# A fused four-layer transformer block: two late weights' lower parts on GpSimd, modulation's products later, new orders for the first five turns

## What is computed

```python
# stage A: per-batch adapter, layer norm with a conditioned bias, then the first half of a DiT block
Wd_b = Wd + 0.1 * (cond @ Wdd.T + bdd).reshape(B, 128, 256)      # a weight of its own for each batch
Wu_b = Wu + 0.1 * (cond @ Wdu.T + bdu).reshape(B, 256, 128)
x = x + relu(x @ Wd_b.T + bd) @ Wu_b.T + bu
x = (layernorm(x) * w + b + tanh(cond @ lin_w.T + lin_b)) * w + b
g1, b1, g2, b2, a1, a2 = split(silu(t + side) @ W_c.T + b_c)      # modulation
q, k, v = split((layernorm(x) * g1 + b1) @ W_qkv.T + b_qkv)       # 16 heads of 16
# stage B: attention over 256 positions
o = softmax(q @ k.T / 4) @ v
# stage C
x = x + (o @ W_o.T + b_o) * a1
x = x + (gelu((layernorm(x) * g2 + b2) @ W_f1.T + b_f1) @ W_f2.T + b_f2) * a2
# stage D: RMS norm, gated GELU, rows quantised to 8 bits, ternary weight
u = (x * scale * rsqrt(mean(x*x) + eps)) @ up_w.T
y = quantise(val * gelu(gate)) @ ternary(down_w).T + x
```

## Time and profile before

| | us |
|---|---|
| median of 3 runs | 933.14 (932.55 to 935.09) |
| the profiled execution | 935.74, its span 933.9 |
| PE busy in the span | 843.1 (90%) |
| DVE, ACT, POOL busy | 565.4, 510.9, 231.2 |
| DMA, mean over the span | 127 GB/s; 344 to 366 in the first 70 us |

### The profile page before, as it was taken

How to read it: one execution, slowest core, us unless ns; L and a number is a source line. 1 busy time by engine, 2 the same in 40 slices (tenths; PEclk the granted TensorE clock), 3 DMA queues, 4 the chain that set the end, 5 groups by cost and what they waited for, 6 DMA issues and landing times.

```text
span 933.9 us, 15916 instructions
## 1 busy us (share of the span) xinstructions
PE 843.1 (90%) x5852; PEld 633.5 (68%) x5852; DVE 565.4 (61%) x1063; ACT 510.9 (55%) x796; POOL 231.2 (25%) x333
## 2 busy tenths in 40 slices
...
GB/s 344 365 366 252 248 138 124 148 80 122 62 203 38 135 97 114 120 78 156 47 187 47 188 47 188 46 173 61 154 76 142 65 127 80 104 80 25 24 12 12
DMA packets 58477, 118.48 MB, mean 127 GB/s; under 512 B 6336, under 2 KB 15936, under 8 KB 55696
## 3 DMA queue, kind: packets, MB, share of 16 engines
...
## 4 chain that ended last, share of the span: by engine, by line
PE 74%; issue 9%; DMA 7%; DVE 4%; ACT 2%; SPq 2%; POOL 2%; POOLq 0%; DVEq 0%; ACTq 0%
PE bank L486 30%; PE bank L692 11%; PE pair_s L653 6%; PE pair_s L618 5%; PE pair_t L639 5%; PE pair_t L486 4%; DMA hyp<-in_hyper 3%; PE bank L737 3%; PE bank L664 3%; PE bank L567 2%; PE bank L729 1%; PE bank L561 1%; DVE oq L1145 1%; DMA wc<-in_cols 1%; PE bank L574 1%
## 5 line engine op out<-in xcount | busy, mean ns | idle before, releaser
L851 ACT ACTIVATE Pr<-pair_t 128x1024 f32<-128x1024 f32 x128 | 131.3, 1026 | 125.2 <-PE pair_t L639 121.5
L1121 DVE TENSOR_REDUCE nmax<-pair_s 128x4 f32<-128x1024 f32 x128 | 155.8, 1217 | 34.5 <-PE pair_s L618 33.9
L692 PE MATMUL bank<-wf,G 128*128 128x256 f32 x512 | 123.0, 387 | 0.1
L486 PE MATMUL bank<-wup_hi,hD_hi 128*128 128x512 f32 x256 | 109.4, 427 | 4.8 <-POOL hD_lo L1316 4.1
L1344 POOL TENSOR_TENSOR x<-x,xcr 128x512 f32<-128x512 f32 x16 | 20.5, 1281 | 358.1 <-DVE x L1179 358.1
L692 PEld LDWEIGHTS bank<-wf,G 128*128 128x128 f32 x512 | 93.3, 190 | 15.5 <-issue 0.2
L486 PE MATMUL bank<-wup_lo,hD_hi 128*128 128x512 f32 x256 | 102.0, 398 | 0.0
L486 PE MATMUL bank<-wup_hi,hD_lo 128*128 128x512 f32 x256 | 101.9, 398 | 0.0
L618 PE MATMUL pair_s<-Kp,Qp 64*128 64x256 f32 x512 | 66.1, 337 | 21.7 <-DVE nmax L1121 13.0
L895 ACT ACTIVATE gl<-bank,rsD 128x512 f32<-128x512 f32 x64 | 44.1, 689 | 63.6 <-PE bank L486 63.4
L1189 DVE SCALAR_TENSOR_TENSOR hd<-bank,rsD,gl 128x512 f32<-128x512 f32 x64 | 47.9, 748 | 46.2 <-PE bank L486 34.7
...
## 6 DMA issues: line engine op xcount, KB each, us to landing
hyp<-in_hyper SPq DMA_DIRECT2D x16, 1024.0 KB, 10.2
...
```

The source lines that it names most:

```text
L486: mm = pe.matmul(dst, l, r, start=first and i == 0, stop=last and i == 2)
L692: mm = pe.matmul(bank[5][:, r * D:(r + 1) * D], G[:, k, r * P:(r + 1) * P], wf2[:, k, :], start=k == 0, stop=k == FT - 1)
L851: act.activation(Pr[:, p % 4, :, :].rearrange("p a n -> p (a n)"), pair_t[:, :, :].rearrange("p a n -> p (a n)"), ACT.Exp, scale=DH ** -0. ...
L1121: dve.tensor_reduce(nmax[:, n % 2, :, p % GP, :], pair_s[:, :, :].rearrange("p a (r n) -> p a r n", r=RT), AX.X, ALU.max, negate=True).the ...
```

## The change

Four things change together. W.fa and W.up's lower parts move from DVE to POOL, in 4 and 8 pieces of 128x512 each. Modulation's products move behind the generation's passes 2 and 3 on PE (wo's product too), and DVE copies slot 3 of the first round earlier. All five lists of turns 0 to 4 are new. SP waits, ahead of A.qs and A.ks in turns 1 to 5, until the head loads of the batch before have landed (`heads_in`), since they read what is overwritten. The diff, the lists of PE, ACT and DVE cut behind turn 2, with which go moves of the same kind: in turns 3 and 4 C.xt is taken at the end of the turn instead of in the next one, A.down and A.up of turn 4 ahead of C.g0 of turn 3, D.quant0 ahead of A.ln in turn 3:

```diff
@@ HEAD["SP"]
-        0: A.load A.qs A.ks A.ql0 A.kl0 A.ql1 A.ql2 A.ql3 A.kl1 A.kl2 W.late A.kl3 1: B.m0 A.load B.m1 A.qs A.ql0 A.ks A.ql1 2: C.tc 1: A.ql2 A.kl0
-        A.kl1 A.ql3 A.kl2 A.kl3 2: B.m0 A.load B.m1 A.qs A.ql0 A.ql1 A.ql2 A.ks A.kl0 A.ql3 3: C.tc 2: A.kl1 A.kl2 3: A.load B.m0 2: A.kl3 3: B.m1
-        A.qs A.ql0 A.ks A.kl0 D.y0 A.ql1 A.ql2 4: C.tc 3: D.y1 A.ql3 A.kl1 A.kl2 4: B.m0 A.load 3: A.kl3 4: A.qs A.ql0 A.ks A.ql1 B.m1 A.ql2 A.kl0
-        A.kl1 A.ql3 A.kl2 D.y0 D.y1 A.kl3""",
+        0: A.load W.late A.qs A.ks A.ql0 A.ql1 A.ql2 A.kl0 A.ql3 A.kl1 A.kl2 1: A.load 0: A.kl3 1: B.m0 B.m1 A.qs A.ql0 A.ks A.ql1 A.kl0 2: C.tc 1:
+        A.ql2 A.kl1 A.kl2 A.ql3 A.kl3 2: B.m0 A.load A.qs B.m1 A.ql0 A.ql1 A.ks A.kl0 A.kl1 A.ql2 A.ql3 3: C.tc 2: A.kl2 3: A.load 2: A.kl3 3: B.m0
+        A.qs A.ql0 A.ks A.ql1 B.m1 A.kl0 A.ql2 4: C.tc 3: D.y0 A.kl1 A.kl2 4: B.m0 3: A.ql3 A.kl3 4: A.qs A.ks B.m1 A.ql0 A.kl0 A.ql1 A.load A.kl1
+        A.ql2 3: D.y1 4: A.ql3 D.y0 A.kl2 D.y1 A.kl3""",
@@ HEAD["PE"]
-        0: A.down A.up W.qkv A.ht A.q A.k A.v 1: A.down A.up B.s0 B.s1 B.s2 B.s3 A.ht B.m0 B.s4 B.s5 B.t0 B.s6 B.t1 B.s7 B.t2 A.q B.m1 A.k B.t3 B.o0
-        B.t4 B.o1 B.t5 A.v B.t6 2: A.down 1: B.t7 B.o2 B.o3 2: A.up C.proj B.s0 B.s1 C.ht B.s2 W.fa W.abs B.s3 C.f0 B.m0 C.f1 B.s4 A.ht C.f2 B.s5 C.f3
+        0: A.down A.up A.ht W.qkv A.q A.k A.v 1: A.down A.up B.s0 B.s1 B.s2 B.s3 A.ht B.m0 B.s4 B.s5 B.t0 B.s6 B.t1 B.s7 B.t2 B.t3 A.q B.m1 A.k B.o0
+        B.o1 B.t4 B.t5 A.v B.t6 W.fa 2: A.down 1: B.t7 2: A.up 1: B.o2 B.o3 2: B.s0 W.abs C.proj B.s1 C.ht B.s2 B.s3 C.f0 B.m0 A.ht B.s4 C.f1 C.f2
...
@@ HEAD["ACT"]
-        0: W.qkv A.down A.lnb A.ht A.q W.fa A.k A.v 1: A.down W.up A.lnb A.ht B.t0 B.t1 A.q B.t2 B.t3 B.t4 A.k B.t5 A.v B.t6 B.t7 2: A.down C.lnb C.ht
+        0: A.down W.qkv A.lnb A.ht W.fa A.q A.k A.v 1: A.down A.lnb W.up B.t0 A.ht B.t1 B.t2 A.q B.t3 A.k B.t4 B.t5 A.v B.t6 2: A.down 1: B.t7 2:
...
@@ HEAD["DVE"]
-        0: W.qkv A.up A.lna A.lng A.ln A.q A.cur A.k 1: A.up A.lna B.s0 A.lng B.s1 A.ln B.s2 B.s3 B.p0 B.m0 B.s4 B.s5 A.cur B.s6 B.s7 B.p1 W.fa B.m1
-        W.up A.q A.k B.o1 W.abs B.o3 2: A.up C.proj C.ln B.s0 B.s1 A.lna A.lng B.s2 A.ln B.s3 B.p0 B.m0 B.s4 B.s5 A.cur B.s6 B.s7 B.p1 A.q A.k B.m1
+        0: A.up A.lna A.lng A.ln W.qkv A.q A.cur A.k 1: A.up A.lna B.s0 A.lng B.s1 A.ln B.s2 B.s3 B.p0 B.m0 B.s4 B.s5 B.s6 B.s7 B.p1 B.m1 W.abs A.q
+        B.o1 A.cur A.k 2: A.up 1: B.o3 2: A.lna C.proj C.ln B.s0 B.s1 A.lng B.s2 A.ln B.s3 B.p0 B.m0 B.s4 B.s5 B.s6 B.s7 B.p1 A.q A.k B.m1 W.tern B.o1
...
@@ HEAD["POOL"]
-        0: A.down A.up A.lna A.ln A.ht 1: A.down A.up A.lna A.ln A.ht 2: A.down C.proj C.ln A.up C.ht A.lna A.ln A.ht 3: A.down 2: C.g3 C.xt 3: C.proj
-        C.ln A.up C.ht A.lna A.ln A.ht 4: A.down 3: C.g3 C.xt 4: C.proj A.up C.ln A.lna C.ht A.ln A.ht C.g3 C.xt""",
+        0: A.down A.up A.lna A.ln A.ht W.fa 1: A.down A.up A.lna A.ln A.ht 2: A.down W.up A.up C.proj C.ln A.lna C.ht A.ln A.ht 3: A.down 2: C.g3 C.xt
+        3: C.proj C.ln A.up A.lna C.ht A.ln A.ht 4: A.down A.up 3: C.g3 C.xt 4: C.proj C.ln A.lna C.ht A.ln A.ht C.g3 C.xt""",
@@ SP, A.qs and likewise A.ks
+                        if 1 <= a <= 5:
+                            for j in range(4):
+                                sp.wait_ge(heads_in[j], 32 * a)
                         sp.wait_ge(act_a, at(ACT_A, "qhi1", a))
@@ PE, ahead of the turns
             generate(0, 1)
+            generate(0, 2)
+            generate(0, 3)
             pe.wait_ge(wc_in, 16)
...
-            generate(0, 2)
             pe.wait_ge(wo_in, 16)
...
-            generate(0, 3)
@@ PE's waits
-                pe.wait_ge(dve_w, at(DVE_W, "f1", 0))
+                pe.wait_ge(pool_w, at(POOL_W, "f1", 0))
...
                 pe.wait_ge(dve_w, len(DVE_W))
+                pe.wait_ge(pool_w, len(POOL_W))
@@ DVE, ahead of the turns
             generated(0, 1)
+            generated(0, 3)
             dve.wait_ge(pre_pe, 3)
...
-            generated(0, 3)
             dve.wait_ge(pre_act, 3)
@@ POOL (the two calls of DVE's low_part for f1 and up go)
+            def split(hi, lo, raw, step_, n):
+
+                pool.wait_ge(act_w, at(ACT_W, step_, 0))
+                width = raw.shape[1] // n
+                flat_hi, flat_lo = (w[:, :, :].rearrange("p k n -> p (k n)") for w in (hi, lo))
+                for i in range(n):
+                    part = slice(i * width, (i + 1) * width)
+                    last = pool.tensor_tensor(flat_lo[:, part], raw[:, part], flat_hi[:, part].bitcast(F32), ALU.subtract)
+                last.then_inc(pool_w, 1)
+
+            def f1_weights():
+                split(wf1_hi, wf1_lo, wf1_raw, "f1", 4)
+
+            def up_weights():
+                split(wup_hi, wup_lo, wup_raw, "up", 8)
```

More of the change, by code:

```diff
@@ L79 @@
-        B.t4 B.o1 B.t5 A.v B.t6 2: A.down 1: B.t7 B.o2 B.o3 2: A.up C.proj B.s0 B.s1 C.ht B.s2 W.fa W.abs B.s3 C.f0 B.m0 C.f1 B.s4 A.ht C.f2 B.s5 C.f3
-        B.t0 B.s6 A.q B.s7 B.t1 A.k B.m1 B.t2 B.o0 A.v B.t3 C.g0 B.t4 C.g1 B.t5 B.o1 B.t6 C.g2 B.t7 C.g3 B.o2 B.o3 3: A.down 2: C.xt 3: B.s0 C.proj
-        W.up B.s1 A.up D.u0 B.s2 D.u1 C.ht B.s3 D.u2 C.f0 B.m0 C.f1 C.f2 B.s4 A.ht C.f3 D.u3 B.t0 B.s5 A.q B.s6 A.k B.t1 B.s7 D.qt0 B.t2 A.v B.m1 B.t3
-        B.o0 4: A.down 3: B.o1 B.t4 C.g0 B.t5 D.y0 D.qt1 B.t6 C.g1 C.g2 B.t7 C.g3 B.o2 B.o3 D.y1 4: B.s0 A.up 3: C.xt 4: C.proj B.s1 D.u0 B.s2 D.u1
@@ new lines @@
+        B.s5 C.f3 B.t0 B.s6 A.q B.s7 B.t1 A.k B.m1 B.o0 B.t2 A.v B.t3 C.g0 B.t4 C.g1 B.t5 C.g2 B.o1 B.t6 C.g3 B.t7 B.o2 B.o3 3: A.down W.up 2: C.xt 3:
+        B.s0 C.proj B.s1 A.up D.u0 B.s2 D.u1 C.ht B.s3 D.u2 C.f0 D.u3 C.f1 B.m0 C.f2 A.ht B.s4 C.f3 B.s5 D.qt0 B.t0 B.s6 A.q B.s7 B.t1 A.k B.t2 A.v
+        B.m1 B.o0 B.t3 4: A.down 3: D.y0 4: A.up 3: C.g0 B.t4 C.g1 B.t5 B.o1 C.g2 D.qt1 B.t6 C.g3 B.t7 D.y1 B.o2 B.o3 C.xt 4: B.s0 C.proj B.s1 D.u0
+        B.s2 D.u1 C.ht B.s3 D.u2 C.f0 B.m0 C.f1 C.f2 A.ht B.s4 C.f3 B.s5 D.u3 A.q B.s6 B.t0 A.k D.qt0 B.s7 B.t1 A.v B.m1 B.t2 C.g0 B.t3 C.g1 B.t4 B.o0
@@ L85 @@
+        B.o1 D.y0 B.t5 C.g2 D.qt1 B.t6 C.g3 B.t7 D.y1 B.o2 B.o3 C.xt""",
     "ACT": """
-        0: W.qkv A.down A.lnb A.ht A.q W.fa A.k A.v 1: A.down W.up A.lnb A.ht B.t0 B.t1 A.q B.t2 B.t3 B.t4 A.k B.t5 A.v B.t6 B.t7 2: A.down C.lnb C.ht
-        A.lnb C.f0 C.f1 A.ht C.f2 C.f3 B.t0 A.q B.t1 A.k B.t2 B.t3 B.t4 A.v B.t5 B.t6 B.t7 C.xt 3: A.down D.u0 C.lnb D.u1 C.ht D.u2 C.f0 A.lnb C.f1
-        A.ht C.f2 C.f3 D.u3 B.t0 A.q B.t1 B.t2 A.k A.v B.t3 4: A.down 3: D.qt0 B.t4 B.t5 B.t6 B.t7 D.qt1 C.xt 4: D.u0 C.lnb D.u1 C.ht D.u2 A.lnb C.f0
@@ L89 @@
-        C.f1 A.ht C.f2 C.f3 D.u3 A.q B.t0 A.k D.qt0 B.t1 B.t2 B.t3 B.t4 D.qt1 B.t5 A.v B.t6 B.t7 C.xt""",
+        0: A.down W.qkv A.lnb A.ht W.fa A.q A.k A.v 1: A.down A.lnb W.up B.t0 A.ht B.t1 B.t2 A.q B.t3 A.k B.t4 B.t5 A.v B.t6 2: A.down 1: B.t7 2:
+        C.lnb C.ht A.lnb C.f0 A.ht C.f1 C.f2 C.f3 B.t0 A.q B.t1 A.k B.t2 A.v B.t3 B.t4 B.t5 B.t6 B.t7 C.xt 3: A.down D.u0 C.lnb D.u1 C.ht D.u2 D.u3
+        C.f0 A.lnb C.f1 A.ht C.f2 C.f3 B.t0 A.q B.t1 A.k B.t2 A.v D.qt0 B.t3 4: A.down 3: B.t4 B.t5 D.qt1 B.t6 B.t7 C.xt 4: D.u0 C.lnb D.u1 C.ht D.u2
@@ L90 @@
+        A.lnb C.f0 C.f1 A.ht C.f2 C.f3 D.u3 A.q B.t0 A.k B.t1 B.t2 D.qt0 B.t3 B.t4 A.v B.t5 D.qt1 B.t6 B.t7 C.xt""",
     "DVE": """
-        0: W.qkv A.up A.lna A.lng A.ln A.q A.cur A.k 1: A.up A.lna B.s0 A.lng B.s1 A.ln B.s2 B.s3 B.p0 B.m0 B.s4 B.s5 A.cur B.s6 B.s7 B.p1 W.fa B.m1
-        W.up A.q A.k B.o1 W.abs B.o3 2: A.up C.proj C.ln B.s0 B.s1 A.lna A.lng B.s2 A.ln B.s3 B.p0 B.m0 B.s4 B.s5 A.cur B.s6 B.s7 B.p1 A.q A.k B.m1
-        W.tern B.o1 C.g3 B.o3 3: B.s0 C.proj B.s1 C.ln A.up D.u0 B.s2 A.lna A.lng D.u1 A.ln B.s3 B.p0 B.m0 D.quant0 B.s4 D.u2 A.cur B.s5 D.u3 B.s6 A.q
@@ L94 @@
-        B.s7 B.p1 B.m1 A.k D.quant1 B.o1 D.y0 C.g3 B.o3 D.y1 4: B.s0 C.proj B.s1 A.up C.ln D.u0 B.s2 A.lna A.lng D.u1 A.ln B.s3 B.p0 B.m0 D.quant0
-        D.u2 B.s4 B.s5 D.u3 B.s6 A.q B.s7 B.p1 A.k B.m1 D.quant1 A.cur B.o1 D.y0 C.g3 D.y1 B.o3""",
+        0: A.up A.lna A.lng A.ln W.qkv A.q A.cur A.k 1: A.up A.lna B.s0 A.lng B.s1 A.ln B.s2 B.s3 B.p0 B.m0 B.s4 B.s5 B.s6 B.s7 B.p1 B.m1 W.abs A.q
+        B.o1 A.cur A.k 2: A.up 1: B.o3 2: A.lna C.proj C.ln B.s0 B.s1 A.lng B.s2 A.ln B.s3 B.p0 B.m0 B.s4 B.s5 B.s6 B.s7 B.p1 A.q A.k B.m1 W.tern B.o1
@@ L96 @@
+        C.g3 A.cur B.o3 3: B.s0 C.proj B.s1 C.ln A.up D.u0 B.s2 A.lna A.lng D.u1 D.quant0 D.u2 A.ln B.s3 B.p0 D.u3 B.m0 B.s4 B.s5 B.s6 A.cur B.s7 A.q
+        B.p1 B.m1 A.k D.quant1 4: A.up 3: B.o1 D.y0 4: A.lna 3: C.g3 D.y1 B.o3 4: B.s0 C.proj B.s1 C.ln D.u0 B.s2 A.lng D.u1 B.s3 A.ln B.p0 D.quant0
+        B.m0 D.u2 B.s4 B.s5 D.u3 B.s6 A.q B.s7 B.p1 A.k B.m1 D.quant1 B.o1 D.y0 C.g3 D.y1 A.cur B.o3""",
     "POOL": """
-        0: A.down A.up A.lna A.ln A.ht 1: A.down A.up A.lna A.ln A.ht 2: A.down C.proj C.ln A.up C.ht A.lna A.ln A.ht 3: A.down 2: C.g3 C.xt 3: C.proj
```

17 lines of the change are left out of this document (7 added, 10 removed).

## The result

| | before | after |
|---|---|---|
| median of 7 runs each, on one chip | 935.09 (932.55 to 935.33) | 939.19 (937.46 to 940.82) |
| ratio | | 1.0051, 95% interval 1.0040 to 1.0062 |
| profiled execution, its span | 935.74, 933.9 | 938.65, 936.9 |
| last pass of the generation | 61.66 | 64.66 |
| C.proj of turn 2, C.f0, C.proj of turn 5 | 140.97, 153.09, 287.34 | 144.39, 156.45, 291.08 |

A forecast was written before the change was run, and what follows sets the result against it. TensorE, busy for 90% of the span and full from C.f0, was taken as the bound, so only turn 5's start counts: 4.7 - 1.3 - 0.8 = +2.6 us, median 933.14 to 935.7, range 928.5 to 940.0.

The forecast's parts named there:

- The generation: Making of per-batch weights ahead of turn 0: its last chunk's pass moves from 61.66 to 66.3 us, +4.7 us.
- T: Moment in the generation when the reload behind the loop's first pass is issued: 39.3 us; no change at 34.7.
- Rival B: Generation: modulation's products run at the upper clock level, 6.2 us for 12.46; time 928.9 us; chance 0.14.
- Turn 0: First turn, after the generation: relu ahead of W.qkv and other moves give -2.9 us, bounds -3.9 and -2.9.
- beside ACT's and POOL's work: Turn 0: W.qkv's lower part, behind A.ln on DVE, runs alongside ACT's and POOL's work; no cost was counted.
- Turns 1 and 2: Stretch up to C.f0, turn 0's gain included: C.f0 1.3 us earlier, between 0.9 and 2.3.
- A.q 121.5 to 124.4: Turn 1 on PE: A.q, waiting for t3, runs from 121.5 to 124.4 us on the clock of the trace before.
- The other arm: Turn 1's chain through q_lo (128.2), k_lo (132.8), its store and load, to B.s0 at 139.7 to 140.6 us.
- Turns 2 to 4: From C.f0 to turn 5: part of PE's idle time is saved, -0.8 us, bounds -2.5 and +3.
- SP's waits for the heads: Turns 1 to 5, ahead of A.qs and A.ks: cost nothing; +3 us if turn 4's wait isn't covered by q_hi's.
- the main case, A: The forecast's steps hold as summed: 933.5 to 938.5 us, chance 0.56.
- rival C: Generation as forecast, but SP's or DVE's waits idle PE in turns 1 to 4: 937.8 to 941 us, chance 0.12.

The follow-up runs named there:

- e5: The kernel after with TensorE's turn-1 order of before (A.q ahead of B.t3, B.t4 between B.o0 and B.o1): 940.0 us, ratio 1.0058.
- e6: The kernel after with ScalarE's turn-1 order of before (W.up ahead of A.lnb, A.ht ahead of B.t0): 940.54 us, ratio 1.0058.
- e8: The kernel after with 9 and 6 idle matmuls behind the generation's passes 1 and 2, ahead of modulation's products: 938.79 us, ratio 1.0051.
- e1: The kernel before with only the generation's new order (passes 2 and 3 ahead of modulation's products, slot 3's copy earlier): 938.26 us, ratio 1.0045.
- e3: The kernel after, with DVE holding W.qkv's lower part back until GpSimd has computed turn 0's roots: 939.04 us, ratio 1.0049.
- e2: The kernel after with the generation's old order, the rest of the change kept: 936.08 us, ratio 1.0022.
- e4: The kernel before with W.fa and W.up's lower parts moved to GpSimd in pieces, plus SP's new waits, orders otherwise of before: 934.02 us, ratio 0.9996.
- f2: e4 with turn 0's part of the change, W.qkv's lower part held back until GpSimd's roots, otherwise before's order: 929.17 us, ratio 0.9934.

## Why the prediction was right in direction and short in size

**The generation: right.** Its model was: the reload behind the loop's first pass at T, the last pass at T + 27. In after, e5, e6 and e8 the distance is 27.1, 27.2, 27.6 and 27.1 us, in e1 and e3 27.0 and 27.2. T was 37.5 in the profiled execution, not 39.3. Of the 1.8 us, 0.8 is the products' start (chunk 3 was there for its pass at 21.77, not at 22.45, one of the signs of being wrong that the text names), 0.7 their length with those behind them (11.8 us for 12.46), and 0.3 wo's product and the first pass, which met the upper level. That made +3.0 there. Over five profiles with the new order (after, e1, e3, e5, e6) the last pass starts at 65.9 in the mean, over four with the old one (before, e2, e4, f2) at 61.5: +4.4, and e1's time says +4.2. The forecast was +4.7. The hole (32 to 39 us for 33 to 41) and the length of the 32 products (7.01 us for 7.0) were as told.

**Rival B: refuted.** The products don't profit from following a pass. In after they ran at 219 ns each from start to end, as before; in e8, begun at the upper level, they lost it 1.8 us in. The rise that "TensorE: Matmul & The Clock Gate" of the Trainium skill, section "What's actually happening", ties to sustained busy time did not come in 7 us of them in any run.

**Turn 0: the step that failed is "beside ACT's and POOL's work".** The relu gave what was forecast. W.qkv's lower part on DVE was put at nothing, but it held GpSimd's root for 1.5 us, on the path to A.ht (e3). The text had named this kind of collision for A.cur in the other direction only. A.cur took 0.65 us more (bound 1.0). Turn 0 gave 1.8 us at A.q and 1.9 at the scores of turn 1 (1.0 to 1.3 there in e2, e5, e6 and e8), not 2.9. With the collision taken out and turn 1 as in before (f2) it gives 3.4 there, so the rest of this step's sum holds. The rule of the Trainium skill's "SBUF — State Buffer", section "Who interferes with whom", that an instruction holds the shared ports to its end, agrees: 1.71 us for an addition of 0.19, ending with DVE's.

**Turns 1 and 2: wrong in sign.** At C.f0 the forecast was -1.3, turn 0's gain included; it is +0.4 (91.8 against 91.4). Of these 1.7 us 1.0 is turn 0's shortfall at the scores. From there to C.f0 the text has +1.6 (-2.9 becomes -1.3) and the traces +2.2: that turn 1 gives back a part of turn 0's gain was foreseen, and 0.6 us too small. Within it the step "A.q 121.5 to 124.4" failed. I had A.q wait for t3, and let t3 come on time; but behind A.ht's two operations on ScalarE the second exponential starts at 122.54, t3 has PE waiting 1.12 us for it and starts at 125.51, and A.q at 126.24, though hA_lo was there at 123.98. Then o0 and o1 (1.93 us) stand ahead of t4, which came at 133.14. On the clock that the prediction uses, 3.0 us less, these are 123.2 for A.q's start, foretold as 121.5, and 130.1 for t4, foretold as 127.9; 1.0 us of each is turn 0's. That o2 now waits behind A.up (0.9 us ahead of C.proj) is not in the text at all. The other arm, that of q_lo and the heads, did move as forecast (first scores of turn 2 at 143.64, counted from the last pass 79.0 against 82.4), but it had stopped being last. That C.f0 came at 156.45, as foretold, is two errors that cancel.

**Turns 2 to 4: -0.8 forecast, +0.4 measured.** From C.f0 to C.proj of turn 5 it is 134.6 us against 134.3, with PE idle for 3.7 and 3.6 us of it; over the kernels without idle matmuls the way took 132.9 to 134.9 us, so neither a gain of 0.8 nor a loss of 0.4 can be told there. SP's waits for the heads did hold it once, in turn 4 (list of SP's waits, 260 to 265 us):

```profile
SPq L431 <- DMA Kp<-qk_scratch: 2.6, 1, 2.6
```

It cost nothing, for the reason that the text gave: behind it SP waited another 4.1 us for q_hi, which ended at 267.71, and its store was issued at 267.80. In e4 the same wait took 4.3 us and the time didn't change.

**The sum.** 4.7 - 1.3 - 0.8 became, in the profiled execution, 3.0 + 0.4 + 0.4, less 0.8 behind turn 5 for which no step stands and which is within the 644.6 to 647.7 us of that stretch: +2.9. That this is so near +2.6 is luck: a generation put 1.7 too high, turns put 2.9 too low and this 0.8 nearly cancel. The medians say 4.1, which fits the mean of the generations, since this execution's was early. 939.19 lies outside the 933.5 to 938.5 of the main case, A, and within the whole range, which reached from 928.5 to 940.0. In time it is rival C (937.8 to 941), and only in part by its mechanism: DVE and GpSimd do collide (turn 0, with GpSimd the one that waits), SP's waits cost nothing, and the rest is the new orders of turns 1 to 4. What each of these costs in time no run shows; f2, with the orders of before behind turn 0, is at -5.9 by the median, where e2, with the new ones and the collision, is at +1.5.
